# Four graph layers on one core: the far-end row spread by transpositions, and the third layer's end weights stacked as high, low, high, low columns

## The reference, cut to what matters

```python
# layer 0, one head
h  = x @ W
s1 = h @ a[:256];  s2 = h @ a[256:]            # two "ends" for every node
e  = leaky_relu(s1[:, :, None] + s2[:, None, :], 0.2)
att = softmax(where(adj > 0, e, NEG), axis=-1)
x  = layernorm(x + elu(att @ h))
# layer 2, four heads of 64
q = (h @ W).reshape(B, N, 4, 64)
e_src = q @ a[:64];  e_dst = q @ a[64:]        # near and far end, per head
e = leaky_relu(e_src[:, :, None, :] + e_dst[:, None, :, :], 0.2)
att = softmax(where(adj > 0, e, NEG), axis=2)
x = layernorm(x + elu(att @ q))
```

## Time and profile before

| | us |
|---|---|
| Runs | 3196.74, 3192.03, 3191.0; median 3192.03 |
| Span of the profiled execution, first to last instruction | 3188.3 |
| Median less span (what lies around the span; the profiled execution's own total isn't listed apart from the runs) | 3.7 |
| Busy shares of the span | PE 90%, PEld 49%, DVE 83%, ACT 85%, POOL 78% |
| Mean granted TensorE clock | 0.969 of full |

### The profile page before, as it was taken

How to read it: one execution, slowest core, us unless ns; L and a number is a source line. 1 busy time by engine, 2 the same in 40 slices (tenths; PEclk the granted TensorE clock), 3 DMA queues, 4 the chain that set the end, 5 groups by cost and what they waited for, 6 DMA issues and landing times. The chain is left out here.

```text
span 3188.3 us, 69772 instructions
## 1 busy us (share of the span) xinstructions
PE 2872.0 (90%) x22768; PEld 1557.5 (49%) x22768; DVE 2654.2 (83%) x7356; ACT 2720.5 (85%) x5847; POOL 2497.3 (78%) x2519
## 2 busy tenths in 40 slices
PE   3899998998999899999989999999999999999865
PEld 3444444544555454555545545554555454454433
DVE  3878887988898798889888987988998798898774
ACT  4768888988998898898989879898998899897874
POOL 4657778878788787888878788887878887886874
PEclk8999999999999999999999999999999999999977
DMA  6435555765656576565757664674655466554453
GB/s 148 97 69 106 121 103 109 144 125 120 130 112 121 117 137 126 120 125 111 134 114 142 125 126 105 124 138 104 147 123 119 106 139 127 120 120 100 100 114 86
DMA packets 1215802, 378.90 MB, mean 119 GB/s; under 512 B 1157712, under 2 KB 1194320, under 8 KB 1215440
## 3 DMA queue, kind: packets, MB, share of 16 engines
q1 hardware_dynamic: 1213616, 373.46, 56.9%
q10 hardware_dynamic: 1824, 0.99, 0.2%
HBM read 21.43 MB, written 16.78 MB: 12 GB/s over the span
## 5 line engine op out<-in xcount | busy, mean ns | idle before, releaser
L855 POOL TENSOR_TENSOR split_r<-prob_r,split_r 128x512 f16<-128x512 f32 x768 | 930.7, 1224 | 214.8 <-DVE split_r L1297 214.7
L1262 DVE CUSTOM_DVE_ANT_0 unused<-bank_ps,neg_mask 128x512 bf16<-128x512 f32 x1024 | 650.1, 682 | 47.6 <-PE bank_ps L1461 43.8
L1526 PE MATMUL bank_ps<-val_r,trans_r 128*128 128x64 f16 (+1 forms) x9216 | 626.1, 221 | 47.1 <-DMA trans_r<-split_r 46.6
L1084 ACT ACTIVATE prob_r<-bank_ps 128x512 f32<-128x512 f32 x1024 | 566.4, 601 | 118.9 <-PE bank_ps L1478 115.2
L1526 PEld LDWEIGHTS bank_ps<-val_r,trans_r 128*128 128x128 f16 x9216 | 522.1, 98 | 296.0 <-issue 122.3
L1247 DVE CUSTOM_DVE_ANT_0 masked_r<-bank_ps,neg_mask 128x512 f32<-128x512 f32 x768 | 508.1, 680 | 127.2 <-ACT bank_ps L1050 98.1
L1297 DVE CAST split_r<-prob_r 128x512 f16<-128x512 f32 x768 | 534.8, 703 | 88.5 <-ACT prob_r L1062 80.0
L1062 ACT ACTIVATE prob_r<-masked_r,low_r 128x512 f32<-128x512 f32 x768 | 557.4, 734 | 56.4 <-DVE low_r L1247 38.5
L1486 PE MATMUL bank_ps<-prob_r,value_ones 128*64 128x512 f32 (+1 forms) x2048 | 552.8, 610 | 2.7 <-ACT prob_r L1084 2.5
L1477 PE MATMUL bank_ps<-stack 98*128 98x512 f16 x1024 | 394.6, 385 | 55.9 <-DVE low_r L1247 19.7
L861 POOL TENSOR_TENSOR split_r<-xcur,split_r 128x512 f16<-128x512 f32 x256 | 300.2, 1186 | 130.6 <-ACT split_r L976 129.9
(11 more groups left out here) (145 smaller groups left out, 4920.4 us busy)
## 6 DMA issues: line engine op xcount, KB each, us to landing
stack<-qk SPq DMA_DIRECT2D x384, 128.0 KB, 2.6
xcur<-in_x_dram SPq DMA_DIRECT2D x32, 512.0 KB, 4.3
out_dram<-z SPq DMA_DIRECT2D x32, 512.0 KB, 3.6
trans_r<-split_r SPq DMA_TRANSPOSE x768, 2.8
xt_r<-split_r SPq DMA_TRANSPOSE x320, 2.8
stack<-low_rows SPq DMA_DIRECT2D x128, 4.0 KB
qk<-in_adj_dram SPq DMA_DIRECT2D x1, 1024.0 KB, 8.1
z<-in_L_gnn_W_dram SPq DMA_DIRECT2D x4, 256.0 KB, 10.1
```

Of the source, the lines that this page charges most:

```text
L855: nc.gpsimd.tensor_tensor(split_r[:, j, 1, :], prob_r[:, i, :], split_r[:, j, 0, :], ALU.subtract).then_inc(lo_done.sem, 1)
L1084: nc.scalar.activation(prob_r[:, entry("prob", "pt", g, *key), :], bank_ps[entry("bank", "u", g, *key)][:], ACT.Exp).then_inc(exp_done.sem, 1)
L1262: nc.vector.tensor_tensor_reduce(out=unused[:, nth % 2, :], in0=bank_ps[entry("bank", "sq", g, t, b, h)][:], in1=neg_mask[:, b, :], scale= ...
L1526: ins = nc.tensor.matmul(bank[:, at:at + width], trans_r[:, i, pp, jb, :], val(g, layer)[:, vp, jb, cols], start=(n == 0), stop=(n == len( ...
```

## The change

It has two parts and what they need.

1. `fb`: the four float32 products with the identity become four transpositions (`nc.tensor.transpose`) of the same broadcast column, into the same place of the same bank. What is computed is the same row.
2. `s2`: the weight tile is now one of 128 columns for each half of the features: high part, low part, high part, low part, 32 columns each. Four products (two halves of the features, high and low activations) fill 128 rows. Rows 0 to 31 and 64 to 95 hold weights' high part times x, rows 32 to 63 and 96 to 127 low part times x. ACT rounds all 128 rows into `far`, and DVE writes the rounding error to rows 64 to 127. `sel_col` and `sel_near` select and sum the four rows of a head, and `bc` and `nr` are 128 rows deep. (The product low x low, left out before, is in the sum now.)

The planner's costs are not changed, so the order of all engines is the same.

```diff
-        sel_col = sb("sel_col", [64, HEADS[2], P], f16)
+        sel_col = sb("sel_col", [P, HEADS[2], P], f16)
-        W["s2"] = sb("w_s2", [P, 2, CT, 64], f16)
+        W["s2"] = sb("w_s2", [P, CT, P], f16)
-        sel_near = sb("sel_near", [64, HEADS[2]], f16)
+        sel_near = sb("sel_near", [P, HEADS[2]], f16)
-        far_r = [sb(f"far{i}", [64, N], f16) for i in range(POOLS["far"])]
+        far_r = [sb(f"far{i}", [P, N], f16) for i in range(POOLS["far"])]
...
@@ POOL, setup (the counts of setup_pool that are waited for grow by 2)
-            for n, at_row in enumerate((0, 32)):
+            for n, at_row in enumerate((0, 32, 64, 96)):
                 nc.gpsimd.affine_select(out=sel_col[:], in_=sel_col[:], ...
@@ ACT
-                        ins = nc.scalar.activation(far(g)[:], bank[0:64, :], ACT.Copy, scale=1.0 / WSCALE)
+                        ins = nc.scalar.activation(far(g)[:], bank, ACT.Copy, scale=1.0 / WSCALE)
@@ DVE, setup
-            after(nc.vector.tensor_copy(stage_s2[:, :, 32:64], stage_s2[:, :, 0:32]))
-            split_weight(W["s2"], stage_s2)
+            for at_col in (0, 64):
+                after(nc.vector.tensor_copy(W["s2"][:, :, at_col:at_col + 32], stage_s2))
+            for at_col in (32, 96):
+                after(nc.vector.tensor_tensor(W["s2"][:, :, at_col:at_col + 32], stage_s2, W["s2"][:, :, 0:32], ALU.subtract))
             split_weight(W["c0"], stage_c0)
-            after(nc.vector.tensor_tensor(sel_near[:], ident32[0:64, HEADS[2]:2 * HEADS[2]],
-                                          ident32[0:64, 32 + HEADS[2]:32 + 2 * HEADS[2]], ALU.add))
+            near_cols = ident32[:].rearrange("p (r c) -> p c r", r=P // 32)[:, HEADS[2]:2 * HEADS[2], :]
+            after(nc.vector.tensor_reduce(sel_near[:], near_cols, mybir.AxisListType.X, ALU.max))
@@ DVE, every graph
-                            dst = other = far(g)[32:64, :]
-                            bank, factor = bank[32:64, :], 1.0
+                            dst = other = far(g)[64:P, :]
+                            bank, factor = bank[64:P, :], 1.0
@@ PE
-                    elif job in ("q", "k", "g", "s2", "f1"):
-                        out_rows = 64 if job == "s2" else P
+                    elif job == "s2":
+                        ops = [(t, xp) for t in range(CT) for xp in range(2)]
+                        for i, (t, xp) in enumerate(ops):
+                            ins = nc.tensor.matmul(bank[:], W[job][:, t, :], turned[:, t, xp, :],
+                                                   start=(i == 0), stop=(i == len(ops) - 1))
+                    elif job in ("q", "k", "g", "f1"):
...
-                        ins = nc.tensor.matmul(bank[:, b * P:(b + 1) * P], ends0[s][:, b, 1:2].broadcast_to([P, P]), ident32[:],
-                                               start=True, stop=True)
+                        ins = nc.tensor.transpose(bank[:, b * P:(b + 1) * P], ends0[s][:, b, 1:2].broadcast_to([P, P]), ident32[:])
```

More of the change, by code:

```diff
@@ L706, in graph_layers_kernel @@
         stage_c0 = xcur[3][:, CT, 0:2 * CT].rearrange("p (t n) -> p t n", t=CT)
-        stage_s2 = xcur[3][:, CT, C // 2:].rearrange("p (t n) -> p t n", t=CT)
+        stage_s2 = xcur[3][:, CT, C // 2:].rearrange("p (t n) -> p t n", t=CT)[:, :, 0:32]
         stage_a0 = z_r[4][:, 0:2, :]
@@ L833, in _ @@
             nc.gpsimd.memset(value_ones[:], 0.0).then_inc(setup_pool, 1)
-            eng.wait_ge(setup_pool, 6)
+            eng.wait_ge(setup_pool, 8)
             nc.gpsimd.memset(stack[len(STACK) * D1:len(STACK) * D1 + 2, :, 1, :, :], 1.0 / LOW_SCALE).then_inc(setup_pool, 1)
-            eng.wait_ge(setup_pool, 7)
+            eng.wait_ge(setup_pool, 9)
             for e in range(2):
@@ L839, in _ @@
                 nc.gpsimd.memset(value_ones[:, :, :, ones_at:ones_at + 1], 1.0).then_inc(setup_pool, 1)
-            eng.wait_ge(setup_pool, 9)
+            eng.wait_ge(setup_pool, 11)
             for n, k in enumerate(SPLIT_ORDER):
@@ L1419, in _ @@
                                                        W[job][:, wp, t, :], start=(i == 0), stop=(i == len(ops) - 1))
-                    elif job in ("q", "k", "g", "s2", "f1"):
-                        out_rows = 64 if job == "s2" else P
+                    elif job == "s2":
[4 more added lines that the diff above has]
+                    elif job in ("q", "k", "g", "f1"):
                         ops = [(wp, xp, t) for t in range(CT) for wp, xp in TERMS]
                         for i, (wp, xp, t) in enumerate(ops):
-                            ins = nc.tensor.matmul(bank[0:out_rows, :], W[job][:, wp, t, n * P:n * P + out_rows], turned[:, t, xp, :],
+                            ins = nc.tensor.matmul(bank[:], W[job][:, wp, t, n * P:(n + 1) * P], turned[:, t, xp, :],
                                                    start=(i == 0), stop=(i == len(ops) - 1))
```

## The result

Nine runs of the changed kernel against nine of the one before, on the same chip: median 3182.73 us (3177.71 to 3186.96) against 3191.0 us, ratio 0.9975 with a 95% interval of 0.9964 to 0.9985. That is 8 us faster, where 14 were forecast (3178.0 us, range 3162 to 3191). The intervals overlap; the gain is 4 to 8 us. Of TensorE work, 32 us were forecast to go; summed over all graphs, from the first start of each of the two steps to the next start behind it, 34 to 35 us went.

What follows compares the result with a forecast made beforehand. No engine was taken as full, PE, ACT and DVE sharing the path. PE loses 14.4 + 18 = 32 us; half of a 28 us ceiling, 14 us, arrives: 3178.0 us, range 3162 to 3191.

Steps and rivals of the forecast that it cites:

- What bounds the kernel: Whole kernel: no engine is full; in one repetition PE is busy 94%, ACT 89%, DVE 87%, and the path changes engines.
- Part 1, size of the step: Far-end row on PE: from 0.89 to 0.98 us down to 0.44 to 0.53, 14.4 us over 32 graphs.
- Part 2, size of the step: Ends of layer 2 on PE: 0.43 us less at full clock, 0.86 at the low one, 18 us in all.
- 10 x 0.86: Ends of layer 2 in the one graph of three at low clock: 0.86 us saved in each of 10 graphs.
- Nothing elsewhere: ACT's rounding, DVE's subtraction, deeper products and the setup's extra selections: taken as no added time, with small bounds.
- From PE time to the end: Whole kernel: of 32 us of PE work removed, 14 us reach the end, between 6 and 28.
- a ceiling of 28 us: Waits behind the changed steps allow 2.57 us per repetition of three graphs, 28 us in all.
- The signs: New profile: PE busy 20 us or more lower, repetition 282.7 us for 284, PE idle per repetition 18.2 to some 20.
- The number: Time of the runs: span 3174.3 us plus 3.7 us for launch and end, 3178.0 us.
- The clock: Rival: transpositions at the far-end step make PE's clock fall more often, 3229 us if at each of 30 steps; 11%.
- Taken up by ACT and DVE: Rival: busy ACT and DVE absorb PE's gain across the graphs, under 6 us arrives, 3188 us; 21%.

Runs made afterwards that it cites:

- the cuts: Changed kernel with some work left out on one engine; ratio to the kernel before: PE 0.9962, ACT 0.998, DVE 0.9966 and 0.9971, POOL 1.0002.
- s2_only: Kernel after with the four float32 far-end products kept, so only the ends of layer 2 changed: 3184.45 us, ratio 0.9981 to the kernel before.
- after_again: The changed kernel unaltered, measured and profiled a second time against the kernel before, five rounds: 3187.88 us, ratio 0.9988.
- fb_only: Kernel before with only the far-end row made by transpositions: 3189.3 us, ratio 0.9992 to the kernel before.
- fb_six: Kernel before with two of its four far-end products made twice, 0.45 us of PE more a graph: 3203.31 us, ratio 1.004.

## Why the prediction was right, and where it was off

- *What bounds the kernel*: no engine is the bound alone. Right, and the cuts show it for each of the four: none gave more than a quarter of the work cut.
- *Part 1, size of the step*: 0.44 to 0.53 us forecast, 0.43, 0.49 and 0.53 measured in the three graphs of a repetition, in place of 0.89, 0.99 and 0.98. Right; 4 records in place of 8.
- *Part 2, size of the step*: 0.43 us less at full clock, 0.86 at the low one; the step alone measured 0.46 (0.40 to 0.56 over the graphs) and 1.01. At full clock that is right: PE's next step behind `h2` comes 0.4 to 0.7 us sooner after the start of `s2`. The term "10 x 0.86" was too large. From `s2` to that next step, the nine graphs in which `s2` took 2.67 us before take 54.6 us in all before, 53.9 and 54.4 in the two profiles of the changed kernel, and 51.8 in `s2_only`: 0.2 to 2.8 us less, where nine times 0.86 is 7.7. The low clock then lay on the products of `h2`, and in some of these graphs PE also waited for DVE's rounding error in `far` (0.81 us at 1339.17, where before there was no wait). For all 32 graphs this stretch is 10 to 15 us shorter (156.8 before; 146.4, 145.4 and 142.1), in place of 18.
- *Nothing elsewhere*: ACT's `far` has a median of 597 ns in place of 591, DVE's subtraction 695 in place of 684, `bc` 379 in place of 376. Within the bounds. In the setup POOL's four selections took 2.97 us in place of 1.40 for two, and POOL still waited 20.66 us for ACT behind them; DVE waited 4.96 us for PE in place of 6.21. Hidden, as forecast; that the first product would start 2 us sooner in both profiles (with the doubts above) wasn't. POOL in the setup of the kernel after:

```profile
1.93 2.97 POOL L829 TENSOR_SCALAR_AFFINE_SELECT sel_col<-sel_col 128x512 f16<-128x512 f16 x4
...
31.75 1.22 POOL L843 TENSOR_TENSOR w_h<-xcur,w_h 128x512 f16<-128x512 f32 x1 [20.66 <-ACT w_h L962]
```

- *From PE time to the end*: this is the term that was too large. I read a ceiling of 28 us from the waits behind the steps and took half of it, for no better reason than that three engines have shares of the same size. Three tenths (8 us), by the second measurement a seventh (4 us), arrived. The ceiling also took each wait for a gain at the end: a wait of 0.81 or 2.48 us says that the engine can start sooner, not that its next releaser lets it go on. The wait of 2.48 us shows it: at the same place of the changed kernel ACT's `far` (1334.31) waits for nothing, and its next operation waits 1.96 us for the first products of `h2`, as it did before (1.92). In `after_again` the two waits are 0.67 and 1.47 us. `fb_only` shows the same for the other step: ACT's waits for this step fell by 7.1 us, the end by 2.6.
- *The shares of the parts*: by the same waits the far-end step has 0.23 + 0.45 us and a part of the 0.79, a quarter to two fifths of the ceiling of 2.57 us. In the parts alone it is 2.6 of 8.7 us. The proportion fits, but with 3 us to either side of each part that can be luck.
- *The signs*: PE's busy time fell by 25 us in `after_again` (20 or more forecast), and its idle time in the window 57 to 2900 rose from 181 to 205 us, from 18 to 20.5 for 284 us, as forecast. A repetition of 282.7 us in place of 284 wasn't confirmed: from the eighth graph's far-end step to the last's, eight repetitions have means of 283.0 us before, 282.5 and 283.8 in the two profiles of the changed kernel.
- *The number*: what lies around the span is 2.1 to 2.4 us in the runs of the kernel before that have both numbers listed, not the 3.7 us of the table, which compares two executions; the forecast, 3192.03 - 14, doesn't depend on it. Both measurements lie within 3162 to 3191, which holds every gain from 1 to 30 us. That the time lies in it says little for the half that was taken.
- *The clock*: the rival fell. The mean clock is 0.969 before and after, and the window 57 to 2900 has 0.98 in both. Four transpositions a graph in place of four products changed nothing there: the product behind them at 1217.02 takes 0.38 us, as its fellow before (1220.60). The rule of the Trainium skill ("TensorE: Matmul & The Clock Gate", Part 4: PE-mode transpose), that transposes don't count as PE-busy in the same way, isn't borne out at the size of this step; no run here tests it with more of them in a row. What I had wrong about the clock is the term of part 2 above.
- *Taken up by ACT and DVE*, 3188 us: it is the second measurement (3187.88), and 5 us off the first, as the forecast is. The two rivals for the time can't be told apart by it. Its mechanism is the one that `fb_only` and `fb_six` show, with the correction that the others aren't full either.

## What to carry to other kernels

In a kernel whose order is fixed and whose engines are balanced, ask of a step not how long it is but how long the next engine waits for it, and then what that engine waits for next: here a saving at one step passed on by about a fifth, while the same cost added there passed on by nine tenths (and twice that cost by seven tenths). Add the cost before you take it away: a run with the step made longer tells whether it is on the path, and its gain when shortened is still another question. Several small cuts on different engines, together, gave here about their sum, and a new order cost more than all of them gave. Don't count a step that runs at the low clock double without a look at what stands behind it: the low clock may lie there once the step is short. And profile the same kernel twice before reading a difference of 10 us in an engine's busy time.

## What the runs showed of the hardware

- A float32 product of 128x128 stands in the trace as two weight loads and two matmul records, the transposition as one of each, at half the time (0.43 against 0.89 us for four).
- Rows cost next to nothing: 128 rows in place of 64 took ACT 597 against 591 ns, and 64 in place of 32 took DVE 695 against 684 ns; a product 128 deep in place of 64 took 379 against 376 ns.
- The low clock can cost the next step what the one before it saves: where `s2` fell from 2.67 to 1.66 us, the `h2` products behind it rose from 2.99 to 4.34 us, and the stretch of both from 5.59 to 6.10, at a mean granted clock of 0.60 in place of 0.72. Over nine such graphs the two together got 0.2 to 2.8 us shorter in three profiles, not nine times 1.01.
- DVE's casts of 512 columns from SBUF to SBUF vary between 0.37 and 1.58 us within one run, with a median of 0.47. Halving 128 of them brought the mean of these from 599 to 608 ns down to 498 (median 427 to 294), and the sum of all 768 is 537.3 and 549.2 us in two profiles of the same kernel.

```profile
L1299 DVE CAST split_r<-prob_r x768: 368/466/1580, 62.8 to 3161.4; 128x512 f16<-128x512 f32 x192
```
